# One instruction per head that adds the attention bias and takes the row maximum

## The reference

```python
qh, kh, vh = (_lora_proj(m, ...).reshape(Bt, S, HEADS, D) for m in (layernorm(x), ctx, ctx))
scores = jnp.einsum('bqhd,bkhd->bhqk', qh * SCALE, kh) + attn_bias
p = jax.nn.softmax(scores, axis=-1)
x = x + jnp.tanh(g_xattn[0]) * jnp.einsum('bhqk,bkhd->bqhd', p, vh).reshape(Bt, S, HEADS * D)
x = x + jnp.tanh(g_ffn[0]) * experts(layernorm(x))   # one expert per token, gelu between two products
```

## Time and profile before

| | |
|---|---|
| time, median of 3 runs | 1298.34 us |
| lowest and highest | 1293.51 and 1300.4 us |
| span of the profiled execution | 1282.7 us |
| TensorE busy | 1264.4 us (99%) |
| VectorE busy | 1098.7 us (86%) |
| GpSimd busy | 1034.5 us (81%) |
| ScalarE busy | 860.4 us (67%) |

### The profile page before, as it was taken

One profiled execution on the slowest core, in us unless ns is written; L12 is line 12 of the kernel. 1 busy time (PEld: TensorE's weight loads), 2 busy tenths in 40 slices (PEclk: granted clock), 3 DMA queues, 4 the chain that ended last, 5 costly groups with the idle time before them and its releaser, 6 DMA issues. The chain is left out here.

```text
span 1282.7 us, 42229 instructions
## 1 busy us (share of the span) xinstructions
PE 1264.4 (99%) x12820; PEld 1078.7 (84%) x12820; DVE 1098.7 (86%) x2504; ACT 860.4 (67%) x1916; POOL 1034.5 (81%) x1179
## 2 busy tenths in 40 slices
PE   8999999999999999999999999999999999999997
PEld 7888888888888888888888888888887788888886
DVE  6899999999999999999999999999999856665655
ACT  4777777777777777777777777777776533333332
POOL 4879989999999999999999999989988755544545
PEclk9999999999999999999999999999999999999999
DMA  6655655556655656555555555555655589888885
GB/s 237 213 179 196 193 187 181 188 186 196 191 185 181 186 187 197 191 192 183 181 185 187 195 193 185 181 184 187 192 195 182 187 271 282 281 278 281 276 281 184
DMA packets 110649, 263.48 MB, mean 205 GB/s; under 512 B 15332, under 2 KB 34278, under 8 KB 110464
## 3 DMA queue, kind: packets, MB, share of 16 engines
q1 hardware_dynamic: 96912, 226.76, 56.6%
q0 software_dynamic: 12624, 34.62, 6.9%
q10 hardware_dynamic: 1056, 1.39, 0.3%
HBM read 226.72 MB, written 36.91 MB: 206 GB/s over the span
## 5 line engine op out<-in xcount | busy, mean ns | idle before, releaser
L455 POOL TENSOR_TENSOR sc<-sc,negmax 128x1024 f32<-128x1024 f32 x256 | 482.4, 1901 | 25.6 <-DVE negmax L1029 20.7
L1023 DVE TENSOR_TENSOR sc<-bank,sc 128x512 f32<-128x512 f32 x512 | 328.2, 683 | 12.3 <-PE bank L560 7.5
L1029 DVE TENSOR_REDUCE negmax<-sc 128x8 f32<-128x1024 f32 x256 | 312.4, 1220 | 16.3
L862 ACT ACTIVATE PT<-bank 128x512 f32<-128x512 f32 x512 | 281.1, 607 | 1.7 <-PE bank L585 1.5
L585 PE MATMUL bank<-cst,sc 128*128 128x128 f32 x2048 | 272.6, 276 | 0.0
L585 PEld LDWEIGHTS bank<-cst,sc 128*128 128x128 f32 x2048 | 225.3, 140 | 25.8 <-issue 25.1
L525 POOL DMA_INDIRECT out<-og,ids x120 | 118.8, 990 | 114.7 <-issue 106.6
L856 ACT COPY OT<-bank 128x512 f32<-128x512 f32 x128 | 75.1, 587 | 152.1 <-PE bank L595 152.0
L510 POOL DMA_INDIRECT rows_dram<-x2n,slot_i x128 | 136.5, 1066 | 29.3 <-issue 25.2
L560 PE MATMUL bank<-KT,QT 32*128 32x256 f32 x2048 | 146.6, 400 | 0.6 <-ACT V L904 0.6
L595 PE MATMUL bank<-PT,V 128*32 128x128 f32 x4096 | 137.6, 275 | 0.3 <-issue 0.3
(11 more groups left out here) (148 smaller groups left out, 2052.0 us busy)
## 6 DMA issues: line engine op xcount, KB each, us to landing
sc<-in_bias SPq DMA_DIRECT2D x256, 512.0 KB, 4.9
w_sb<-in_w SPq DMA_DIRECT2D x69, 257.0 KB, 3.9
CT<-in_w SPq DMA_DIRECT2D x69, 256.0 KB, 4.1
xg<-rows_dram SPq DMA_DIRECT2D x63, 272.0 KB, 3.8
x_sb<-in_x SPq DMA_DIRECT2D x128, 128.0 KB, 2.0
CT<-in_ctx_in SPq DMA_DIRECT2D x64, 256.0 KB, 5.4
rows_dram<-x2n,slot_i POOLq DMA_INDIRECT x128, 3.8
out<-og,ids POOLq DMA_INDIRECT x120, 4.0
```

Of the source, the lines that this page charges most:

```text
L455: nc.gpsimd.tensor_tensor(s, s, m, ALU.add).then_inc(sub_ok, 1)
L862: nc.scalar.activation(PT[:, t.slot(2), 512 * q:512 * q + 512], turn_bank(t, q)[:], ACT.Exp).then_inc(pt_ready, 1)
L1023: nc.vector.tensor_tensor(s, b_s[q][:], s, ALU.add).then_inc(s_used, 1)
L1029: nc.vector.tensor_reduce(negmax[:, t.slot(2), 8 * h:8 * h + 8], sc[:, t.slot(4), 1024 * h:1024 * h + 1024].rearrange("p (h k) -> p h k", ...
```

## The change

The adds and the reductions of a sequence are replaced by 16 instructions, one per head: each adds 128 columns of a bank to the bias, writes the sum back to `sc` and the maximum over the 128 columns to one column of `rowmax`. The maximum is no longer negated, so GpSimd subtracts it. GpSimd waits for `s_used` (eight heads done) in place of `max_ok`, which is gone. The wait for `sub_ok` moves from the first reduction to ahead of the first head. A nop stands behind the waits of each group of four heads, and the last head of four counts `s_used` up.

```diff
-        negmax = sb("negmax", [P, 2, HEADS])
+        rowmax = sb("rowmax", [P, 2, HEADS])
...
             def subtract_max(t, h):
-                pool.wait_ge(max_ok, t.n(2, h + 1))
+                pool.wait_ge(s_used, t.n(4, 2 * h + 2))
                 s = sc[:, t.slot(4), 1024 * h:1024 * h + 1024].rearrange("p (h k) -> p h k", h=8)
-                m = negmax[:, t.slot(2), 8 * h:8 * h + 8].unsqueeze(2).broadcast_to([P, 8, P])
-                nc.gpsimd.tensor_tensor(s, s, m, ALU.add).then_inc(sub_ok, 1)
+                m = rowmax[:, t.slot(2), 8 * h:8 * h + 8].unsqueeze(2).broadcast_to([P, 8, P])
+                nc.gpsimd.tensor_tensor(s, s, m, ALU.subtract).then_inc(sub_ok, 1)
...
             def add_bias(t, q):
                 if q == 0:
                     dve.wait_ge(bias_in[t.slot(4)], t.per(4, 32, 32))
+                    if t.reached(2):
+                        dve.wait_ge(sub_ok, t.n(2, -2))
                 dve.wait_ge(s_ready, t.n(4, q + 1))
-                s = sc[:, t.slot(4), 512 * q:512 * q + 512]
-                nc.vector.tensor_tensor(s, b_s[q][:], s, ALU.add).then_inc(s_used, 1)
-
-            def row_max(t, h):
-                dve.wait_ge(s_used, t.n(4, 2 * h + 2))
-                if h == 0 and t.reached(2):
-                    dve.wait_ge(sub_ok, t.n(2, -2))
-                nc.vector.tensor_reduce(
-                    negmax[:, t.slot(2), 8 * h:8 * h + 8],
-                    sc[:, t.slot(4), 1024 * h:1024 * h + 1024].rearrange("p (h k) -> p h k", h=8),
-                    AX.X, ALU.max, negate=True).then_inc(max_ok, 1)
+                dve.nop(nofuse=True)
+                for h in range(4 * q, 4 * q + 4):
+                    s = sc[:, t.slot(4), P * h:P * h + P]
+                    ins = nc.vector.tensor_tensor_reduce(
+                        out=s, in0=b_s[q][:, P * (h % 4):P * (h % 4) + P], in1=s, scale=1.0, scalar=LOWEST,
+                        op0=ALU.add, op1=ALU.max, accum_out=rowmax[:, t.slot(2), h:h + 1])
+                ins.then_inc(s_used, 1)
...
-                    add_bias(cur, 0)
-                    add_bias(cur, 1)
-                    row_max(cur, 0)
-                    add_bias(cur, 2)
-                    add_bias(cur, 3)
-                    row_max(cur, 1)
+                    for q in range(4):
+                        add_bias(cur, q)
```

More of the change, by code:

```diff
@@ L39 @@
 TO_FT = float(3 << 30)
+LOWEST = -3.4028234663852886e38
 CELL = 32
@@ L253, in flamingo_block @@
         q_ready, q_evac, k_ready, k_evac = sem("q_ready"), sem("q_evac"), sem("k_ready"), sem("k_evac")
-        s_ready, s_used, max_ok, sub_ok = sem("s_ready"), sem("s_used"), sem("max_ok"), sem("sub_ok")
+        s_ready, s_used, sub_ok = sem("s_ready"), sem("s_used"), sem("sub_ok")
         tr_ready, pt_ready = sem("tr_ready"), sem("pt_ready")
```

## The result

The changed kernel takes 1350.72 us (median of 4 runs, 1348.66 to 1353.62), the kernel before 1297.1 us (4 runs, 1293.51 to 1300.4): a ratio of 1.0416, 95% interval 1.0394 to 1.0438. It is slower by 4.2%, where 1.5% was forecast, and the rows do not show the reason that the prediction gave. Lines of the changed kernel ahead of `add_bias` stand one higher than before (the scores are L561, the values' product L596, the scatter L511), the heads are L1028.

What follows compares the result with a forecast made beforehand. TensorE and VectorE, both nearly full and handing over once per sequence, were taken to bound the kernel. A later second-bank release added 0.15 us per sequence, 19.5 us over 128, to the median 1298.3: 1318 us, range 1305 to 1340.

Steps and rivals of the forecast that it cites:

- TensorE's own step: Attention stage: without waits for VectorE, four steps take 30.59 us against 30.88, leaving 9 us over 128 sequences.
- the longer circle: Scores, VectorE's second-bank release, projection, next scores: a plain step bound to 7.73 us, where it took 7.44.
- the wider range: 1288 to 1385 us, leaving out the second rival alone; the forecast's own range was 1305 to 1340.
- the prediction's sum: Total time worked out from the price per head: 1318 us at 0.28; each 0.01 us moves it about 12 us.
- The price per head: VectorE, attention stage: 0.21 us for the sum plus 0.07 for writing the maximum, 0.28 us instead of 0.313.
- the second rival: VectorE's sums and write-outs do not overlap: 0.35 to 0.45 us per head, +130 to about +330 us; chance 0.20.
- the first rival: TensorE decides the attention step: at 0.21 us per head the circle is 7.17 us, total 1289 us; chance 0.25.
- The 19.5 us that the forecast added: Attention stage: 0.15 us more per sequence over 128 sequences, from four steps at 31.49 us against 30.88.
- GpSimd costed at nothing: GpSimd's subtractions: same shape, second half may start at 4.48 us instead of 5.00, last in no loop wait.
- third: At 0.25 to 0.27 us per head the longer circle eats TensorE's slack and the time stays; chance 0.12.

Runs made afterwards that it cites:

- the run of adds alone: The kernel before without its two reductions, the maximum left out and GpSimd adding zeros: 1330.07 us.
- half of the heads: The kernel after with the scatter waiting for the values' product, and heads for the first two banks only, old adds and one reduction for the others: 1289.21 us.
- the run with the early scatter: The kernel before with GpSimd's scatter moved up right behind the two subtractions: 1310.07 us.

## Why the prediction was wrong

**What was right.** Most of the reading of what bounds the kernel: TensorE's own step of 7.60, 7.45 and 8.11 us is the floor, and 9 us or so are all that less work on VectorE can give. The runs without collisions and without the stop at the branch come to that floor, at 1283 to 1291 us. The direction came out by luck: the longer circle that was to make the kernel slower is not there. That the measured time lies inside the wider range of 1288 to 1385 is luck too: by the prediction's sum, 1350 us stand for about 0.305 us per head. One figure of that sum is off, without bearing on the forecast: 0.32 us per head give some +71 us and not +85.

**The price per head.** The prediction took 0.28 us, 0.21 for the sum and 0.07 for writing the maximum out. Measured are 0.21 us from start to start, and 0.20 with no maximum at all. This step failed too: a term of 0.07 us where the runs show none. The sum's price came out of the earlier trace rows to the hundredth; the term for the write-out is nothing, the lower bound. The instructions of the earlier trace rows that were taken for it have inputs to read; the accumulator read has none, and starts together with the next sum. The rule on the drain that the second rival cited (the Trainium skill, "VectorE: DVE Perf Modes", section "The DRAIN you can't avoid": the next op starts only when the pipe is empty) does not hold between heads: 0.29 us long, they start 0.21 us apart. That section itself excepts a next op that is not held.

**The circle over the second bank.** With 0.21 us it is 7.17 us, below TensorE's step, as the first rival worked out. In the kernel after, one projection waits for VectorE between 200 and 900 us. The 19.5 us that the forecast added have therefore no part in the 53.6 that were lost.

**GpSimd costed at nothing.** This is the step that failed and that set the time. The prediction said of GpSimd's second half that it "may start at 4.48 us instead of 5.00 after the first add; it isn't last in any wait of the loop". Both are true of who waits for GpSimd; what it triggers by being earlier was left out, and so put at nothing. In its place the runs show the scatter on the products: 90 of 110 signals late, and 49 us that come back when one wait moves it off them. The 0.5 us were too small as well: GpSimd's second subtraction starts 2.1 us earlier (7.22 us after the step's scores before, 5.12 after; medians of 200 to 900 us). A row of the waits of 200 to 900 us of the kernel before, which was not among those that the prediction read, shows that VectorE's reductions did hold GpSimd back, once in four steps:

```profile
POOL sc L455 <- DVE negmax L1029: 6.0, 23, 0.3
```

The 0.27 us ahead of the subtraction at 608.32 is one of these waits. Small as they are, they show that GpSimd ran close behind the reductions. From 200 to 900 us its first subtraction starts 5.36 us after the step's scores before the change, 3.27 after, and 2.79 in the run of adds alone, which has no reductions (medians). Its scatter stands 2.7 to 3.0 us behind the end of the second subtraction in all three, so it came forward with them. Against the product it moved by 3.12 - 0.44 = 2.7 us, from the projections onto the products: 2.1 us of this are the earlier subtraction, and most of the rest is the longer step, since the scatter falls into the next one. No row of before has an engine that waits for the scatter; what it does to a product's signal could be read in no row of before, since there 166 signals of projections were due under a scatter and none was late.

**The rivals.** The first had the price and the circle right, and its 1289 us is what comes out with the scatter out of the way and no loop (1290.96), or with half of the heads (1289.21). The second and third fall with the price. A rival in which less work makes another engine's transfer collide was not among them.

**What stays open.** That a scatter under way delays the signal is shown by its place, which five edits changed in kernels with and without heads. What in the chip holds it back is not shown. The matmuls whose own signals were seen late use 32 columns of the array: products and the gate. The scores, which use 32 rows, were on time where the records tell it (20 signals due under a scatter in the kernel after, 40 in the run of adds alone); in the run with the early scatter one first bank of 56 was late. Of the transposes on the full array 83 of 436 were late in the kernel after, all of them started within 1.03 us behind a product's last matmul, 81 of these behind a late one; with the scatter on transposes alone none of those with a record was late. Why records are missing while a scatter is under way, and what stopped TensorE inside the products of that run, is open too. Whether the part of the array is the reason was not tried by itself. Nor was the length between 350 and 470 records at which the stop behind a branch sets in; that the length of the loop is the cause fits every run, but no run lengthened a loop without changing its instructions.

## What to carry to other kernels

When an edit makes an engine's result come sooner, list everything that the next engine then does sooner, DMAs that nobody waits for included, and look what they will lie beside; an engine that waited 6 us in 700 for that result still moved by 2 us. When a kernel gets slower while every engine gets idler, look for a late signal: compare, pair by pair, the time from an instruction to its waiter's start. And count the instructions of an unrolled loop before making one into many: here the branch back cost 3 us with 470 records in the loop.

## What was not expected of the hardware

- While an indirect DMA was being issued by GpSimd (1.07 us), the signals of products on 32 columns came 0.4 to 1.1 us late, most of them 0.2 to 0.5 us behind its end; those full-array projections and transposes by themselves that have a record were on time.
- With that DMA on the scores, TensorE stopped inside 52 of 115 products and went on 0.20 to 0.28 us behind the DMA's end.
- The read of an accumulator cost nothing between heads (0.21 us apart with a maximum, 0.20 without).
- The branch back of VectorE's loop cost 0.3 us with up to 350 records in the loop, and 2.8 to 3.2 us with 470; straight code of the same steps did not stop.
- A VectorE operation of 32 columns with both inputs in SBUF took 2.92 us instead of 0.19 beside two GpSimd subtractions.
